# Small inputs packed into the constants and asked for after the embedding's first part; warm-up products on a preamble constant

## What is computed

```python
h = einsum('bnd,ed->bne', patchify(x), W_proj) + b_proj + pos_emb     # 576 x 768 times 768 x 256
h = concatenate([cls_tok, h], axis=1)                                 # 16 x 37 x 256
h = h + attention(layernorm(h), W_qkv, b_qkv, W_out, b_out)           # causal, 16 heads
z = layernorm(h)
logits = (z @ w_red) @ (wg / maximum(norm(wg), 1e-4)).T               # which of 8 experts
h = h + score * (gelu(z @ w1[e] + b1[e]) @ w2[e] + b2[e])             # e = argmax of the logits
```

## Time and profile before

| | |
|---|---|
| median of 3 runs | 133.79 us (133.21 to 134.04) |
| the profiled execution: time, span | 133.21 us, 131.3 us |
| PE busy | 123.1 us, 94% of the span |
| DVE, ACT, POOL busy | 44%, 37%, 31% |
| DMA: moved | 33.37 MB, mean 254 GB/s |

### The profile page before, as it was taken

How to read it: one execution, slowest core, us unless ns; L and a number is a source line. 1 busy time by engine, 2 the same in 40 slices (tenths; PEclk the granted TensorE clock), 3 DMA queues, 4 the chain that set the end, 5 groups by cost and what they waited for, 6 DMA issues and landing times.

```text
span 131.3 us, 2718 instructions
## 1 busy us (share of the span) xinstructions
PE 123.1 (94%) x1034; PEld 105.2 (80%) x1034; DVE 58.2 (44%) x179; ACT 48.2 (37%) x143; POOL 41.1 (31%) x52
## 2 busy tenths in 40 slices
PE   5999999999999999999899999999999999999960
PEld 1768897887667777777799998999998989999840
DVE  1231899363986898888957000522102121220210
ACT  0300002383866745662349360066042331506000
POOL 8800034850092193314847500050020202011022
PEclk9999999999999999999999999999999999999999
DMA  4899999159469999999996548999999994000000
GB/s 125 276 394 407 379 411 403 56 176 182 96 138 185 242 362 387 364 386 358 400 352 248 228 124 229 355 405 371 397 362 386 350 377 143 24 0 24 2 28 30
DMA packets 19934, 33.37 MB, mean 254 GB/s; under 512 B 1799, under 2 KB 13704, under 8 KB 19918
## 3 DMA queue, kind: packets, MB, share of 16 engines
q1 hardware_dynamic: 18382, 30.73, 70.8%
q0 software_dynamic: 768, 2.12, 4.3%
q10 hardware_dynamic: 768, 0.31, 0.9%
HBM read 27.75 MB, written 5.84 MB: 256 GB/s over the span
## 4 chain that ended last, share of the span: by engine, by line
PE 68%; DMA 14%; DVE 7%; issue 4%; POOL 3%; SPq 2%; ACT 1%; POOLq 0%
PE ps L793 22%; PE ps L807 19%; PE ps L524 9%; DMA w2s<-v_scratch 5%; DMA early<-embed_in 4%; DMA v_scratch<-hz 4%; PE ps L584 4%; PE ps L591 3%; POOL vbd L1118 2%; PE ps L672 2%; PE ps L685 2%; PE ps L715 2%; PE ps L654 1%; SPq L341 1%; PE ps L776 1%
## 5 line engine op out<-in xcount | busy, mean ns | idle before, releaser
L507 ACT ACTIVATE early<-ps,b1s 128x128 f32<-128x128 f32 x64 | 18.2, 370 | 31.7 <-PE ps L793 31.7
L793 PEld LDWEIGHTS ps<-early,w1s 128*128 128x128 f32 x256 | 29.4, 192 | 0.4 <-issue 0.2
L793 PE MATMUL ps<-early,w1s 128*128 128x128 f32 x256 | 29.6, 275 | 0.0
L807 PE MATMUL ps<-w2s,early 128*128 128x256 f32 x128 | 28.8, 379 | 0.0
L807 PEld LDWEIGHTS ps<-w2s,early 128*128 128x128 f32 x128 | 23.8, 190 | 2.9
L524 PE MATMUL ps<-early 128*128 128x256 f32 x60 | 15.4, 408 | 0.5 <-DMA early<-embed_in 0.5
L524 PEld LDWEIGHTS ps<-early 128*128 128x128 f32 x60 | 11.8, 204 | 3.5 <-DMA early<-embed_in 1.8
L1051 DVE COPY early<-ps 128x256 f32<-128x256 f32 x6 | 2.5, 425 | 25.9 <-PE ps L776 25.9
L1143 POOL DMA_INDIRECT out<-pos,early x4 | 3.9, 970 | 25.7 <-DVE pos L1067 25.3
L1143 POOL DMA_INDIRECT out<-pos,wide x4 | 3.9, 973 | 21.1 <-DVE pos L1067 21.1
L591 PE MATMUL ps<-xnt,wqkv 128*128 128x296 f32 x32 | 9.1, 422 | 0.0
(11 more groups left out here) (132 smaller groups left out, 168.1 us busy)
## 6 DMA issues: line engine op xcount, KB each, us to landing
w1s<-w SPq DMA_DIRECT2D x8, 1024.0 KB, 10.7
w2s<-w SPq DMA_DIRECT2D x8, 1024.0 KB, 12.2
slot_scratch<-nil SPq DMA_DIRECT2D x1, 2560.0 KB, 15.1
early<-embed_in SPq DMA_DIRECT2D x5, 448.0 KB, 7.2
early<-slot_scratch SPq DMA_DIRECT2D x4, 320.0 KB, 5.4
wide<-slot_scratch SPq DMA_DIRECT2D x4, 320.0 KB, 6.6
b2s<-b SPq DMA_DIRECT2D x4, 256.0 KB, 8.0
wqkv<-w_qkv SPq DMA_DIRECT2D x1, 768.0 KB, 10.7
```

The source lines that it names most:

```text
L507: nc.scalar.activation(gt[:, t % 2, f, :], ps[:, 2 * (t % 2) + f // 4, (f % 4) * P:(f % 4 + 1) * P], ACT.Gelu, bias=b1t[:, f:f + 1]).then_ ...
L793: m = nc.tensor.matmul(ps[:, 2 * (t % 2) + f // 4, (f % 4) * P:(f % 4 + 1) * P], w1s[:, r, k, f * P:(f + 1) * P], xt[:, t % 2, k, :], star ...
L807: m = nc.tensor.matmul(ps[:, 4 + t % 2, 0:D], gt[:, t % 2, f, :], w2s[:, r, f, :], start=(f == 0), stop=(f == FT - 1))
```

## The change

1. `bqk`, `bv` and `boutc` are written into eight new columns of the constants (`cf` grows by 8 columns of 4 bytes, 4 KB in all). Their three transfers, tiles and semaphores go, and who waited for them waits for `loaded_cf`, or not at all where that was waited for before.
2. ACT waits for `loaded_emb[0]`, the first part of the embedding's first chunk, and only then asks for `cf`, `wgs`, `wredt`, `bproj`, in this order (`cf` and `wgs` are swapped).
3. The warm-up products read `one`, the constant 1.0 in bf16 that POOL writes in the program's preamble, spread over 128x128 and 128x512 by a step of zero. PE doesn't wait for DVE's memset any more, and there are five products in place of four.

```diff
-WARM = 4
+WARM = 5
...
-                  ("patch", NT)):
+                  ("patch", NT), ("bqk", 2 * D // P), ("bv", D // P), ("boutc", D // P)):
...
+        bqk, bv, boutc = C("bqk"), C("bv"), C("boutc")
...
-        bqk = sb("bqk", [P, 2 * KD])
-        bv = sb("bv", [P, KD])
-        boutc = sb("boutc", [P, KD])
...
-        blank = nil[:, 0:D].bitcast(BF16)
+        one = nc.const_aps.tensor(1.0, (P, 1), BF16)
...
         def _(act):
+            act.wait_ge(loaded_emb[0], 16)
+            act.dma_start(cf[:, :], cf_d).then_inc(q["loaded_cf"], 16)
             act.dma_start(wgs[:, :], wg).then_inc(q["loaded_wg"], 16)
-            act.dma_start(cf[:, :], cf_d).then_inc(q["loaded_cf"], 16)
             act.dma_start(wredt[:, :], w_red_t).then_inc(q["loaded_wred"], 16)
             act.dma_start(bproj[:, :], b_proj).then_inc(q["loaded_bproj"], 16)
-            act.dma_start(bqk[:, :], b_qk).then_inc(q["loaded_bqk"], 16)
-            act.dma_start(bv[:, :], b_v).then_inc(q["loaded_bv"], 16)
-            act.dma_start(boutc[:, :], b_out_c).then_inc(q["loaded_boutc"], 16)
...
-            act.wait_ge(q["loaded_bv"], 16)
+            act.wait_ge(q["loaded_cf"], 16)
...
-            pe.wait_ge(q["blank_ready"], 1)
             for _ in range(WARM):
-                nc.tensor.matmul(ps[:, BZ, :], blank[:, 0:P], blank, start=True, stop=True)
+                nc.tensor.matmul(ps[:, BZ, :], one.to_broadcast([P, P]), one.to_broadcast([P, 2 * D]), start=True, stop=True)
...
-                    pe.wait_ge(q["loaded_boutc"], 16)
+                    pe.wait_ge(q["loaded_cf"], 16)
...
-            V.memset(nil[:, 0:2 * D], 0.0).then_inc(q["blank_ready"], 1)
+            V.memset(nil[:, 0:2 * D], 0.0)
...
-            dve.wait_ge(q["loaded_bqk"], 16)
```

More of the change, by code:

```diff
@@ L121, in constants, with vit_tower @@
     return cf, cb.astype(np.dtype("bfloat16")), iota
-def vit_tower(nc, embed_in, places_in, b_proj, w_qkv, b_qk, b_v, w_out, w_out_t, b_out, b_out_c, wg, w_red_t, w1, b1, w2, b2,
+def vit_tower(nc, embed_in, places_in, b_proj, w_qkv, w_out, w_out_t, b_out, wg, w_red_t, w1, b1, w2, b2,
               cf_d, cb_d, iota_d, out):
@@ L279, in o_bank @@
             return BO if u < LAST - 1 else LAST - u
-        names = """loaded_rest loaded_pos loaded_bproj loaded_iota pos_ready loaded_cf loaded_cb loaded_wqkv loaded_wout loaded_bqk
-            loaded_bv loaded_bout loaded_b1 loaded_b2 loaded_wg loaded_wred
+        names = """loaded_rest loaded_pos loaded_bproj loaded_iota pos_ready loaded_cf loaded_cb loaded_wqkv loaded_wout
+            loaded_bout loaded_b1 loaded_b2 loaded_wg loaded_wred
             embedded h_saved veps_ready rstd_ready xn_ready xnt_ps xnt_ready vrow_ps vrow_ready vrow_stored
             wg_sq wg_norm wgn_ready wgnt_ps wgnt_ready wred_ready g_ps bqs_ready
-            qk_ps k0_ready k1_ready q0_ready q1_ready v_zeroed v_ready pads_ready blank_ready wg_ready
+            qk_ps k0_ready k1_ready q0_ready q1_ready v_zeroed v_ready pads_ready wg_ready
             scores_ps shifted_ready lg_ready probs_ready probst_ps probst_ready o_ps o_ready ot_ps ot_ready
             hb_ready proj_ps veps2_ready rstd2_ready shift2_ready h2_ready z_pool z_act
-            loaded_woutt loaded_boutc gc_ready wg_ps hg_ready
+            loaded_woutt gc_ready wg_ps hg_ready
             hot_ready keyu_ready esum_ready score_ready cum_ps place32_dve
@@ L1189 @@
     cf, cb, iota = constants()
+    for name, v in (("bqk", bqkv[0:2 * KD]), ("bv", bqkv[2 * KD:]), ("boutc", a["L0_attn_b_out"].reshape(KD, P))):
+        cf[:, slice(*_F[name])] = v.T
     arrays = {
@@ L1194 @@
         "w_qkv": a["L0_attn_W_qkv"][:, order],
-        "b_qk": bqkv[0:2 * KD].T,
-        "b_v": bqkv[2 * KD:].T,
         "w_out": a["L0_attn_W_out"],
@@ L1199 @@
         "b_out": a["L0_attn_b_out"],
-        "b_out_c": a["L0_attn_b_out"].reshape(KD, P).T,
         "wg": a["L0_ffn_wg"],
```

## The result

| | before | changed |
|---|---|---|
| median | 133.55 us (133.0 to 134.43, 6 runs) | 139.42 us (136.33 to 140.24, 6 runs) |
| the profiled execution: time, span | 133.21, 131.3 us | 139.62, 137.8 us |

The change makes the kernel slower. The changed kernel's six executions fall into two groups: 136.33 and 137.28, and four from 139.21 to 140.24.

What follows compares the result with a forecast made beforehand. It took the kernel to be bound by embedding chunk 1's load until 7.34 us, then by PE; chunk 1 starting at 6.90 instead of 7.38 gave 133.79 - 0.48 = 133.3 us, range 132.6 to 134.3.

Steps and rivals of the forecast that it cites:

- taken at 7.4 us, at worst 8.8: Gate's side calculation: `wgs`, behind `cf`, lands at 7.4 us, 8.8 by `wredt`'s row; `wgn` at 8.94, 0.4 us cover.
- the 5.0 to 6.6 forecast: Embedding chunk 1 lands between 5.0 and 6.6 us, before PE is ready, so PE's wait of 0.29 us goes.
- The 0.07 us for the first part: Chunk 0's first part lands 0.07 us earlier, between nothing and 0.11, with ACT's queue held back.
- The term of 0.12 us: Earlier warm-up makes TensorE's clock rise earlier during chunk 0: 0.12 us taken, half of a possible 0.23.
- the sum: Start of chunk 1 on PE: 3.57 - 0.07 + 3.52 - 0.12 = 6.90 us against 7.38.
- The gain of 0.48 us: PE starts chunk 1 0.48 us earlier, between 0.29 and 0.63, and the total falls by as much.
- The sum's lower end for the clock: Start of chunk 1 with clock and first part unchanged: a gain of 0.29 us.
- The rival of the capped gain: Clock rises no earlier, zero-step operands cost, or chunk 5 isn't earlier: gain 0 to 0.25 us, 133.7 us; chance 0.18.
- The rival on the other side: At L538 PE stalls on late `wgs`: landing at 8.8, `wgn` at 10.34, 0.53 us later, 134.3 us; chance 0.22.
- The lids on the gain: Chunk 5's landing and the second tile's normalising before PE's transposes cap the gain at 0.6 to 0.9 us.
- clearing the slots: `nil_ready` at 9.2 us delays SP's L331 by a quarter of a microsecond, which costs nothing.
- a shift at 20 us: PE's move of the transposes at 20.82 us should arrive at the end unless somebody else is late.

Runs made afterwards that it cites:

- the wait-only kernel: The kernel before with only ACT's wait on the embedding's first part ahead of its seven requests, in the old order: 138.95 us, ratio 1.0274.

## Why the prediction was wrong, point by point

The step that failed is the landing of `cf` and `wgs`: taken at 7.4 us, at worst 8.8, it measured 11.17, and the stall of 2.99 us that follows from it set off a fall of the clock, which had no term at all.

**The start.** PE's first product at 0.77, the warm-up over at 3.06 and in nobody's way; the stationary and the moving operand with a step of zero cost nothing (2.29 us for five, by 1.89 for four). Chunk 1 landed at 6.36, inside the 5.0 to 6.6 forecast, and PE went into it without a gap. These steps held. The 0.07 us for the first part didn't come: it landed 2.78 us after its issue, against 2.8 before, and chunk 0 began at 3.56, against 3.57.

**The clock's rise.** The term of 0.12 us failed. Chunks 0 and 1 took 6.41 us where the sum had 3.40 + 2.43 = 5.83, so PE came to the turning at 9.97, not 9.33, and even later than the 9.81 of before. The gain of 0.48 us would have been gone without any stall. The sum's lower end for the clock was a rise when it came before. The rival of the capped gain did name a later rise, but priced it as no loss; here it cost 0.6 us against the sum.

**`cf` and `wgs`.** This is the step that decided it. I took 3.3 us for `cf`, the row of a request made at 1.35 with nearly nothing ahead, and 4.9 as the upper bound, `wredt`'s. The landing was at 11.17, 7.64 us after the issue. By the traces' packets the 4.3 us more are two parts: the first packet came 3.74 us after the issue instead of 1.85 in the kernel before (I had put it at about one), and from there to the landing it took 3.9 us instead of 1.4. The first part is the wait behind SP; what made the second longer isn't shown. Rows nearer to the case stood in the same list of DMA issues of the kernel before, and I left them out because nobody waited for those transfers:

```profile
bproj<-b_proj ACTq DMA_DIRECT2D x1, 128.0 KB, 6.5
...
bqk<-b_qk ACTq DMA_DIRECT2D x1, 2.0 KB, 7.2
bv<-b_v ACTq DMA_DIRECT2D x1, 1.0 KB, 7.9
boutc<-b_out_c ACTq DMA_DIRECT2D x1, 1.0 KB, 8.9
```

They were asked for at 2.23, 2.70, 3.18 and 3.71, and the time to landing grows by about 1.6 us with each microsecond, down to 1 KB that took 8.9 us. `boutc`, asked for 0.2 us after the moment at which the change asks for `cf`, landed at 12.6. SP's own chunks 4 and 5, asked for at 3.1 and 3.5, took 7.9 and 8.6 us. The series holds more than SP's queue, for the last three stood behind `bproj`'s 128 KB on ACT's own queue as well, so it isn't the price of `cf`, which had nothing of ACT's ahead; in the changed kernel `wredt` and `bproj`, asked for later still, at 4.71 and 5.08, took 6.8 and 8.1 us. But as an upper bound it was there: continued, it puts a small transfer asked for at 3.9 near 13, and that was the bound to take.

**The rival on the other side.** "`wgs` late, PE stalls at L538" was the right mechanism, with the right formula: a landing at 11.17 puts `wgn` at 12.71 (measured 12.90) and PE 2.9 us behind 9.81, thus 136.7 against the lower group's 136.33 and 137.28. But I priced it at a landing of 8.8, 134.3, gave it 0.22, and let that price be the range's end. The mis-sized term is the landing, by 2.4 us against that price and by 3.8 against the 7.4 of the sum.

I put a rule of the Trainium skill ("DMA: Bandwidth & Descriptors", Queues, rings and completion order) against the worst of it, by which each DMA engine alternates between queues by packets, so that ACT needn't wait for SP's backlog. What I drew from it the trace contradicts: for 3.7 us after the issue not one of ACT's packets was moved, with SP's running all the time. Only from the first packet on do both queues move packets, 392 and 296 up to 11.2 us.

**What the stall sets off.** I priced a microsecond of stall at a microsecond. In the profiled execution 3.0 us of idling cost 3.3 us more by the clock, and by their mean clock three more of the six are like it. The Trainium skill ("TensorE: Matmul & The Clock Gate", HAM oscillation) tells of idle gaps that bring the lower clock back; this trace agrees, with the granted clock at 0.50 from 14.1 to 20.9 us.

**What held behind.** The lids on the gain never came into play, clearing the slots was issued at 13.07 and nobody missed it, and a shift at 20 us did arrive at the end undiminished: 6.47 us there, 6.5 in the span.

## What to carry to other kernels

Before a small load is moved behind a larger stream, look in the list of DMA issues at what the transfers asked for at that moment took, on every queue, also those that nobody waits for: the time to landing goes far more by the moment of asking, and by what is asked for ahead, than by the size, and here it rose from 3.3 to 8.9 us within 2.4 us. Then ask which in-order engine stands behind it; if that is TensorE, price the idle time with a possible fall of the clock on top. Only what isn't needed until much later (here `bproj`) can wait.

## What the runs showed of the hardware

A request on ACT's queue waited 1.9 to 3.7 us for its first packet, depending on how much SP had outstanding, and landed 4.0 to 7.6 us after its issue; SP's own request for the same data behind its first two chunks, made 1.4 us earlier, landed 5.0 us after its issue. Unread products of ones by a step of zero gave the same time as those of zeros (133.37 and 133.53 us). After 3.0 us without a product TensorE started again at its higher clock and fell to the lower one 1.2 us later, for 6.8 us, busy all the time; after 3.8 us in the wait-only kernel it fell 0.3 us later, for 3.4 us; after 1.0, 1.5 and 2.1 us the profiles show no fall.
